# A two-layer attention and expert kernel: the expert table's bounds are read between pieces of expert 0, and the output table is cleared in two parts

## The chip, the core and the metric

One core of a Trainium2 chip runs the whole program in one launch. The metric is the device time of an execution in microseconds. Engines: PE is TensorE, DVE is VectorE, ACT is ScalarE, POOL is GpSimd, SP is SyncE, which only issues DMAs. A "q" behind an engine's name (ACTq, SPq, PEldq) stands for its sequencer, the part that takes instructions in order, does register work and passes the others on.

## The reference, cut to what matters

```
x = x + tanh(g_xattn[0]) * L0_xattn(layernorm(x), ctx)     # attention, 16 heads, 77 keys
x = x + tanh(g_ffn[0])   * L0_ffn(layernorm(x))            # 8 experts, each token goes to 2
x = x + tanh(g_xattn[1]) * L1_xattn(layernorm(x), ctx)
x = x + tanh(g_ffn[1])   * L1_ffn(layernorm(x))            # a Fourier-domain linear map

L0_ffn: probs = softmax(x @ gate_w.T); topw, sel = top_k(probs, 2); topw /= sum(topw)
        hact = up * gelu(gate)        # gate, up = x @ gate_up_w[e].T, 2 x 1024 columns
        out  = sum over the token's experts of topw * (hact @ down_w[e].T)
```

x is 16 batches of 256 rows of 256 numbers, so 4096 tokens; which expert gets how many is known only at run time.

## The kernel before, in words

**Layer 0.** Each engine runs a software pipeline over the 16 batches (`steps`). While a batch's attention runs, the one before gets its expert choice, and GpSimd scatters its rows (`scatter`, line 657) into the DRAM table `expert_in` (`xs_d`), where each expert has an area of its own. The DRAM table `expert_out` (`ys_d`, 14336 rows of 1 KB) takes the experts' results. It has to hold finite numbers everywhere, so SyncE clears it in layer 0: each of the 16 steps issues one DMA of 896 rows (`clear`, line 531) from the zeroed tile `zeros`. In SyncE's queue it stands behind `spread` and in front of `keep` (x1 to DRAM, line 554), `base` and `load`.

**The border.** VectorE counts the rows of each expert and writes `tbl`, one row of integers: the first tile of each expert (`bound`), where its whole tiles end and its half tiles begin (`end`), the row of its padding, and its first row in `expert_out` (`offset`); then it signals `tiles_counted` (line 1330). A whole tile is 256 rows, a half tile 128. Loops over tiles have bounds that must be in registers: `value_load` reads one number of `tbl` from SBUF into a register of one engine. In the kernel before, TensorE (lines 1791, 1793), ScalarE (965 to 970) and VectorE (1406 to 1409) each read all that they need for all 8 experts here, 16, 25 and 17 numbers, before their first tile. SyncE reads one padding row and issues `pad_first` (256 zero rows behind expert 0's rows, line 444), waits for all scatters and for `first_padded`, reads expert 0's three bounds (`tile_rows`, 570 to 572) and fetches the first tile (line 576).

**Experts.** A tile: TensorE turns it (`t_x`, line 1758, the transposes of line 1456), ScalarE writes its high half to 16-bit numbers (`x_hi`, line 926), VectorE the rest (`x_low`, line 1360). Then 8 pieces `fc`: `up` (line 1773, 12 matmuls), gelu on ScalarE (947), product and the split in two 16-bit parts on VectorE (1382, 1386, 1388), and two pieces later `down` (1786, 6 matmuls). The next tile is turned within this one, after piece 2's `up`. Within an expert's first two tiles ScalarE and VectorE also convert the next expert's weights, in parts (`next_high`, 938, behind the gelu of pieces 0 to 5 of the first tile; `next_low`, 1371, one for each of pieces 1 to 6 of both), and GpSimd fetches the weights of the one after that as stages come free. The first two tiles of an expert are written out one by one, the rest are loops over a register. The result rows go to `expert_out` from ScalarE's DMA queue (960, 963).

GpSimd, between layer 0 and its weight loop: after the first tile landed it fetches expert 1's down weights (line 737), after the second it runs `pad(pool, 1, E)`, seven DMAs of 256 zero rows. SyncE waits for these before expert 1's first tile.

After expert 7 layer 1 gathers rows from `expert_out` and goes on batch by batch; TensorE is its busiest engine too.

Of the kernel before, what the change touches and what calls it, by code (L numbers as in the profile page):

```python
# [26 lines left out]
P = 128  # L27
NB, S, D = 16, 256, 256
# [3 lines left out]
QT = S // P  # L32
HC = H // KC
E, F = 8, 1024
FC = F // P
TILES = 2 * NB + 4 * E
SHORT = 7
OUT_ROWS = (2 * NB + 3 * E) * S
CAP = NB * S + S
SCALE = 64.0  # L40
INV = 1.0 / SCALE
# [98 lines left out]
def build(nc, a, out):  # L140
# [27 lines left out]
    with ExitStack() as ctx:  # L168
# [3 lines left out]
        def sem(name):  # L172
            return ctx.enter_context(nc.semaphore(name))
# [178 lines left out]
        s.normed_after_turned = sem("normed_after_turned")  # L352
        s.normed_after_high = sem("normed_after_high")
        s.table_zeroed = sem("table_zeroed")
        s.logits = sem("logits")
        s.picked = sem("picked")
        s.prefix = sem("prefix")
# [120 lines left out]
        def _(sp):  # L478
# [51 lines left out]

            def clear(b):

                n = OUT_ROWS // NB
                dst = ys_d[bass.ds(b.i * n, n), :].rearrange("(p t) d -> p t d", p=P)
                sp.dma_start(dst, zeros[:, 0:1].to_broadcast([P, n // P, D])).then_inc(s.table_zeroed, 16)

            def step0(b, front, tail, pre, ld):
                if isinstance(b.i, int) and b.i == 1:
# [27 lines left out]
            keep(at(0, 15))  # L566


            def tile_rows(e):
                t0 = sp.value_load(tbl[0:1, bass.ds(e, 1)], min_val=0, max_val=TILES)  # L570
                t1 = sp.value_load(tbl[0:1, bass.ds(e + 1, 1)], min_val=1, max_val=TILES)
                tw = sp.value_load(tbl[0:1, bass.ds(e + (2 * E + 1), 1)], min_val=1, max_val=TILES)
                with sp.Fori(t0, tw) as g:
                    sp.wait_ge(s.tile_turned, g + 1)
                    row = tile_row(e, g, t0)
                    sp.dma_start(xs, rows(xs_d, row)).then_inc(s.tile_in, 16)
                with sp.Fori(tw, t1) as g:
                    sp.wait_ge(s.tile_turned, g + 1)
                    row = half_row(e, g, t0, tw)
                    sp.dma_start(xs[:, 0], xs_d[bass.ds(row, P), :]).then_inc(s.tile_in, 16)  # L580

            sp.wait_ge(s.tiles_counted, 1)
            pad_first(sp)
            for k in range(2):
                sp.wait_ge(s_scat[k], 64 * (NB // 2))
# [45 lines left out]
        def _(pool):  # L631
# [127 lines left out]
        def _(act):  # L759
# [182 lines left out]
            def expert_tile(e, g, par, part, first, t0, tw, n=QT):  # L942

                for fc in range(FC):
                    act.wait_ge(s.gate_up, g * FC + (fc + 1))
                    act.wait_ge(s.product, g * FC + (fc + 7))
                    act.activation(ge[:, fc % 2, 0:n * P], bank[1 + fc % 3][:, 0:n * P], ACT.Gelu,  # L947
                                   scale=INV).then_inc(s.gelu, 1)
                    if part == 0 and par is not None and fc < 6:
                        next_high(e, par, fc)  # L950
                x_hi(g + 1)
                act.wait_ge(s.down, g * FC + 2 * FC)
                act.wait_ge(s.expert_rows_stored, g * 16 + 16)
                for t in range(n):
                    act.activation(ysb[:, t], bank[4 + t][:, 0:D], ACT.Copy,
                                   scale=INV).then_inc(s.expert_rows, QT // n)
                act.wait_ge(s.expert_rows, g * 2 + 4)
                if n == QT:
                    row = out_row(first + (g * S - t0 * S), S)
                    act.dma_start(rows(ys_d, row), ysb).then_inc(s.expert_rows_stored, 16)  # L960
                else:
                    row = out_row(first + (g * P + tw * P - t0 * S), P)
                    act.dma_start(ys_d[bass.ds(row, P), :], ysb[:, 0]).then_inc(s.expert_rows_stored, 16)

            bound = [act.value_load(tbl[0:1, e:e + 1], min_val=4 if e else 0, max_val=TILES)
                     for e in range(E + 1)]
            end = [act.value_load(tbl[0:1, 2 * E + 1 + e:2 * E + 2 + e], min_val=3, max_val=TILES - 1)
                   for e in range(E)]
            offset = [act.value_load(tbl[0:1, 3 * E + 1 + e:3 * E + 2 + e], min_val=0,
                                     max_val=OUT_ROWS - SHORT * P) for e in range(E)]  # L970

            def expert(e, par):
                t0, t1, tw, first = bound[e], bound[e + 1], end[e], offset[e]
                expert_tile(e, t0, par, 0, first, t0, tw)
                expert_tile(e, t0 + 1, par, 1, first, t0, tw)
                with act.Fori(t0 + 2, tw) as g:
                    expert_tile(e, g, par, 2, first, t0, tw)
                with act.Fori(tw, t1) as g:
                    expert_tile(e, g, par, 2, first, t0, tw, 1)
# [34 lines left out]
        def _(dve):  # L1014
# [361 lines left out]
            def expert_tile(e, g, par, part, n=QT):  # L1376

                q = n * P
                done = part * (12 - sum(LOW_PIECES[1]))
                for fc in range(FC):  # L1380
                    dve.wait_ge(s.gelu, g * FC + (fc + 1))
                    dve.scalar_tensor_tensor(a32[:, fc % 2, 0:q], bank[1 + fc % 3][:, S:S + q], INV,  # L1382
                                             ge[:, fc % 2, 0:q], ALU.mult, ALU.mult).then_inc(s.product, 1)
                    dve.wait_ge(s.product, g * FC + (fc + 9))
                    dve.wait_ge(s.down, g * FC + (fc + 5))
                    dve.tensor_copy(act16[:, fc % 4, 0, 0:q], a32[:, fc % 2, 0:q]).then_inc(s.activation, 1)  # L1386
                    dve.wait_ge(s.activation, g * (2 * FC) + (2 * fc + 1))
                    dve.tensor_tensor(act16[:, fc % 4, 1, 0:q], a32[:, fc % 2, 0:q],  # L1388
                                      act16[:, fc % 4, 0, 0:q], ALU.subtract).then_inc(s.activation, 1)
                    if part < 2 and par is not None:  # L1390
                        for k in range(done, done + LOW_PIECES[part][fc]):
                            next_low(e, par, k)
                        done += LOW_PIECES[part][fc]
                x_low(g + 1)

            def expert(e, par):
                t0, t1, tw = bound[e], bound[e + 1], end[e]
                expert_tile(e, t0, par, 0)
                expert_tile(e, t0 + 1, par, 1)
                with dve.Fori(t0 + 2, tw) as g:  # L1400
                    expert_tile(e, g, par, 2)
                with dve.Fori(tw, t1) as g:
                    expert_tile(e, g, par, 2, 1)

            dve.wait_ge(s.tiles_counted, 1)
            bound = [dve.value_load(tbl[0:1, e:e + 1], min_val=4 if e else 0, max_val=TILES)
                     for e in range(E + 1)]
            end = [dve.value_load(tbl[0:1, 2 * E + 1 + e:2 * E + 2 + e], min_val=3, max_val=TILES - 1)
                   for e in range(E)]
            x_low(0)  # L1410
            for e in range(E - 1):
                expert(e, (e + 1) % 2)
# [38 lines left out]
        def _(pe):  # L1451
# [326 lines left out]
            def down(par, g, fc, w=QT):  # L1778
                if fc == 0:
                    pe.wait_ge(s.expert_rows, g * 2 + 2)  # L1780
                for n, (i, j) in enumerate(PASSES):
# [3 lines left out]
                    for t in range(w):  # L1785
# [5 lines left out]
            bound = [0] + [pe.value_load(tbl[0:1, e:e + 1], min_val=1, max_val=TILES)  # L1791
                           for e in range(1, E + 1)]
            end = [pe.value_load(tbl[0:1, 2 * E + 1 + e:2 * E + 2 + e], min_val=1, max_val=TILES)
                   for e in range(E)]
# [116 lines left out]
```

## Time and profile before

| | |
|---|---|
| median of 3 runs | 1301.15 us (1299.22 to 1301.48) |
| the profiled execution | 1300.25 us, its span 1298.7 us |
| TensorE's matmuls | 1189.8 us busy, 92% |
| VectorE / ScalarE / GpSimd | 69% / 44% / 20% |
| DMA over the span | 119.58 MB, 92 GB/s |
| layer 0 / experts / layer 1 | to about 380 / 380 to about 974 / to the end |

The profile is of one execution. Matmul ends are modelled, so a busy TensorE isn't TensorE at its peak. In a row such as `415.88 3.93 PE bank L1773 x36` the first number is the start in us from the span's start, the second the duration; `L1773` is the line of the kernel. `[0.31 <-DVE tiles L1386]` is idle time before an instruction and what ended it; "issue" is a wait for nothing that the profile shows. A row of a stretch, such as `410.00:415.00 5.00, 5.00 (x46) ...`, gives its length, the busy us of PE, PEld (weight loads), DVE, ACT and POOL with their instructions, TensorE's granted clock (1.00 is 2.4 GHz, 0.50 is 1.2 GHz), the DMA engines' busy share and GB/s.

### The profile page before, as it was taken

How to read it: one execution, taken by the hardware profiler on the slowest of the kernel's cores; microseconds unless marked ns; L12 is line 12 of the kernel's file. 1: busy time of each engine (PE TensorE's matmuls, PEld its weight loads, DVE VectorE, ACT ScalarE, POOL GpSimd, SP SyncE). 2: the span in 40 equal slices, each digit the busy share in tenths (PEclk: the TensorE clock that was granted, in tenths of full speed). 3: DMA queues.
4: the chain of work that ended last, by engine and by line, in shares of the span. 5: the costliest groups of instructions: out<-in, count | busy, mean ns of one | idle time of the engine just before them, and what ended most of it. 6: DMA issues, size and time to landing. Idle time of an engine off the chain costs nothing.

```text
span 1298.7 us, 34926 instructions
## 1 busy us (share of the span) xinstructions
PE 1189.8 (92%) x11816; PEld 992.6 (76%) x11816; DVE 892.5 (69%) x2696; ACT 569.6 (44%) x1184; POOL 263.2 (20%) x394
## 2 busy tenths in 40 slices
PE   4898989898867999999999999999997999999996
PEld 3677777776646888888888888888885777777774
DVE  4687677777645667675766767686565787787872
ACT  4565555555513242242424233242223665666652
POOL 5023242333331000000000000000004344444310
PEclk9899788888878999999999999999999999999998
DMA  9443333333433213021121313101012232222210
GB/s 293 183 162 107 117 116 124 128 101 110 150 133 138 91 37 127 33 95 61 71 94 38 122 34 126 34 25 46 26 47 81 66 93 87 81 82 85 82 34 21
DMA packets 82745, 119.58 MB, mean 92 GB/s; under 512 B 27326, under 2 KB 52558, under 8 KB 80589
## 3 DMA queue, kind: packets, MB, share of 16 engines
q1 hardware_dynamic: 64172, 60.32, 14.8%
q0 software_dynamic: 12848, 49.05, 11.3%
q10 hardware_dynamic: 5616, 8.78, 1.8%
q8 instruction: 66, 1.08, 0.3%
q14 instruction: 43, 0.34, 0.1%
HBM read 63.81 MB, written 47.58 MB: 86 GB/s over the span
## 4 chain that ended last, share of the span: by engine, by line
PE 80%; DVE 7%; issue 6%; SPq 2%; ACT 2%; DMA 1%; another core or an unknown queue 0%; POOL 0%; DVEq 0%; POOLq 0%; ACTq 0%
PE bank L1773 28%; PE bank L1786 14%; PE bank L1600 7%; PE bank L1534 6%; PE bank L1456 5%; PE bank L1587 3%; PE bank L1517 3%; PE bank L1519 3%; PE bank L1476 3%; PE bank L1540 2%; PE bank L1611 1%; DVE bm L1094 1%; PE bank L1598 1%; PE bank L1560 1%; PE bank L1502 1%
## 5 line engine op out<-in xcount | busy, mean ns | idle before, releaser
L1773 PE MATMUL bank<-tiles,we 128*128 128x256 f16 (+1 forms) x3744 | 392.6, 258 | 11.1 <-issue 10.2
L1773 PEld LDWEIGHTS bank<-tiles,we 128*128 128x128 f16 x3744 | 324.7, 98 | 51.1 <-issue 18.6
L947 ACT ACTIVATE tiles<-bank 128x256 f32<-128x256 f32 (+1 forms) x312 | 109.3, 353 | 330.9 <-PE bank L1773 312.2
L1786 PE MATMUL bank<-we,tiles 128*128 128x256 f16 x1608 | 223.5, 273 | 5.5 <-DVE tiles L1386 4.4
L1382 DVE SCALAR_TENSOR_TENSOR tiles<-bank,tiles 128x256 f32<-128x256 f32 (+1 forms) x312 | 120.2, 385 | 143.6 <-ACT tiles L947 138.6
L1786 PEld LDWEIGHTS bank<-we,tiles 128*128 128x128 f16 x1608 | 148.7, 98 | 40.8 <-DVE tiles L1386 17.0
L1534 PE MATMUL bank<-qT,kbd 128*128 128x256 f16 x960 | 161.6, 288 | 1.9 <-issue 1.2
L1094 DVE TENSOR_REDUCE bm<-bank 128x4 bf16<-128x308 f32 x256 | 118.2, 475 | 62.9 <-PE bank L1519 48.8
L471 DVE TENSOR_TENSOR pr<-pr 128x512 f16<-128x512 f32 x160 | 108.4, 682 | 30.9 <-ACT pr L809 25.0
L1388 DVE TENSOR_TENSOR tiles<-tiles 128x256 f16<-128x256 f32 (+1 forms) x312 | 121.1, 388 | 11.2 <-DVE tiles L1386 0.7
L1534 PEld LDWEIGHTS bank<-qT,kbd 128*128 128x128 f16 x960 | 97.4, 104 | 21.5 <-issue 1.8
L808 ACT ACTIVATE pr<-bank 128x512 f32<-128x512 f32 x160 | 95.9, 599 | 18.2 <-PE bank L1540 12.3
L1386 DVE CAST tiles<-tiles 128x256 f16<-128x256 f32 (+1 forms) x312 | 85.8, 275 | 24.6 <-DVE tiles L1382 0.2
L417 POOL TENSOR_TENSOR cell<-cell 1x1 f32<-1x1 f32 x81 | 24.4, 306 | 368.7 <-DMA expert_out<-tiles 167.8
L1517 PE MATMUL bank<-kbd,qT 128*128 128x308 f16 x256 | 79.2, 313 | 21.1 <-issue 9.4
L809 ACT ACTIVATE pr<-bank 128x512 f16<-128x512 f32 x160 | 96.8, 605 | 0.0
L1540 PE MATMUL bank<-mrhs,mhead 112*128 112x256 bf16 x320 | 92.1, 288 | 1.7
L1587 PEld LDWEIGHTS bank<-vbd,pr 128*128 128x128 f16 x1920 | 73.8, 99 | 16.5 <-issue 7.6
L1587 PE MATMUL bank<-vbd,pr 128*128 128x34 f16 (+1 forms) x1920 | 79.2, 185 | 7.5 <-issue 7.4
L1519 PE MATMUL bank<-bm,identb 128*128 128x308 bf16 x256 | 79.9, 316 | 0.9 <-issue 0.9
L668 POOL DMA_INDIRECT yg<-expert_out,slot x64 | 63.0, 985 | 35.8 <-issue 16.6
L657 POOL DMA_INDIRECT expert_in<-h,slot x64 | 64.5, 1008 | 20.9 <-issue 16.8
(196 smaller groups left out, 1678.2 us busy)
## 6 DMA issues: line engine op xcount, KB each, us to landing
expert_out<-zeros SPq DMA_DIRECT2D x16, 896.0 KB
wes<-in_guT POOLq DMA_DIRECT2D x9, 1024.0 KB, 5.1
tiles<-expert_in SPq DMA_DIRECT2D x29, 256.0 KB, 2.6
pr<-in_guT POOLq DMA_DIRECT2D x7, 1024.0 KB
yg<-in_dnT POOLq DMA_DIRECT2D x7, 1024.0 KB
expert_out<-tiles ACTq DMA_DIRECT2D x28, 256.0 KB, 2.3
expert_in<-zeros POOLq DMA_DIRECT2D x8, 640.0 KB, 13.0
xin<-in_x SPq DMA_DIRECT2D x16, 256.0 KB
```

The lines of the kernel that those rows point to most:

```text
L471: eng.tensor_tensor(pr[:, g, 1], pr32[:, (b.par + g) % 2], pr[:, g, 0], ALU.subtract).then_inc(low_done(b, g)[0], 1)
L947: act.activation(ge[:, fc % 2, 0:n * P], bank[1 + fc % 3][:, 0:n * P], ACT.Gelu, scale=INV).then_inc(s.gelu, 1)
L1094: dve.tensor_reduce(bm[:, t, MROW + 4 * q:MROW + 4 * q + 4], a_place(g).rearrange("p (h k) -> p h k", h=4), AX, ALU.max).then_inc(s.maxima, 1)
L1382: dve.scalar_tensor_tensor(a32[:, fc % 2, 0:q], bank[1 + fc % 3][:, S:S + q], INV, ge[:, fc % 2, 0:q], ALU.mult, ALU.mult).then_inc(s.prod ...
L1388: dve.tensor_tensor(act16[:, fc % 4, 1, 0:q], a32[:, fc % 2, 0:q], act16[:, fc % 4, 0, 0:q], ALU.subtract).then_inc(s.activation, 1)
L1517: pe.matmul(dst, qT[:, b.par, 0, q // 2, t * P:(t + 1) * P], kbd[:, b.par, 0, q // 2, 4 * (q % 2):4 * (q % 2) + 4], start=True, stop=False)
L1519: pe.matmul(dst, identb[:], bm[:, t, 0:S2].unsqueeze(1).to_broadcast([P, 4, S2]), start=False, stop=True).then_inc(s.top_scores, 1)
L1534: pe.matmul(b_s[(b.par + g) % 2][:, j * S:(j + 1) * S], kbd[:, b.par, ki, c].rearrange("p h k -> p (h k)")[:, start:start + P], qT[:, b.pa ...
L1540: return pe.matmul(b_s[(b.par + g) % 2][:, j * S:(j + 1) * S], mhead[:].rearrange("p h k -> p (h k)")[:, c * ROWS + start:c * ROWS + start ...
L1587: last = pe.matmul(dst, pr[:, g, pi, j * S + t * P:j * S + (t + 1) * P], vbd[:, b.par, c, vi, n0:n1].rearrange("p n d -> p (n d)"), start= ...
L1773: last = pe.matmul(bank[1 + fc % 3][:, half * S:half * S + w * P], gate_up[:, par, c, i, col:col + P], xT[:, j, c, 0:w * P], start=n == 0, ...
L1786: last = pe.matmul(bank[4 + t][:, 0:D], act16[:, fc % 4, i, t * P:(t + 1) * P], we[:, par, 2, j, fc * D:(fc + 1) * D], start=fc == 0 and n ...
```

## The change

It does three things. (1) `bound[0]` is the constant 0, and TensorE, VectorE and ScalarE read the other numbers one at a time by `next_bound()`, called between the pieces of expert 0's first two tiles. (2) SyncE reads expert 0's three bounds before `pad_first` instead of after the waits. (3) Layer 0 clears only the rows that expert 0 can write (17 x 256 = 4352), in 16 clears of 256 rows and one more after the steps; GpSimd issues the other 9984 rows as three DMAs of 3328 rows, after the second tile has landed and before its pads. ScalarE waits for these before expert 1.

```diff
+FIRST_ROWS = NB * S + S
+LATE_CLEARS = 3
 # SyncE
             def clear(b):
-                n = OUT_ROWS // NB
-                dst = ys_d[bass.ds(b.i * n, n), :].rearrange("(p t) d -> p t d", p=P)
-                sp.dma_start(dst, zeros[:, 0:1].to_broadcast([P, n // P, D])).then_inc(s.table_zeroed, 16)
+                sp.dma_start(rows(ys_d, b.i * S), zeros[:]).then_inc(s.table_zeroed, 16)
...
+            sp.dma_start(rows(ys_d, NB * S), zeros[:]).then_inc(s.table_zeroed, 16)
             sp.wait_ge(s.tiles_counted, 1)
+            first = tile_bounds(0)          # the three value_loads that stood in tile_rows
             pad_first(sp)
             for k in range(2):
                 sp.wait_ge(s_scat[k], 64 * (NB // 2))
             sp.wait_ge(s.first_padded, 16)
-            tile_rows(0)
+            tile_rows(0, first)
             sp.wait_ge(s.padding_zeroed, 16 * (E - 1))
             with sp.Fori(1, E) as e:
-                tile_rows(e)
+                tile_rows(e, tile_bounds(e))
 # GpSimd
             pool.wait_ge(s.tile_in, 32)
+            n = (OUT_ROWS - FIRST_ROWS) // LATE_CLEARS
+            for k in range(LATE_CLEARS):
+                dst = ys_d[FIRST_ROWS + k * n:FIRST_ROWS + (k + 1) * n, :].rearrange("(p t) d -> p t d", p=P)
+                pool.dma_start(dst, zeros[:, 0:1].to_broadcast([P, n // P, D])).then_inc(s.later_table_zeroed, 16)
             pad(pool, 1, E)
 # ScalarE
-            act.wait_ge(s.table_zeroed, 16 * NB)
+            act.wait_ge(s.table_zeroed, 16 * (NB + 1))
...
                     if part == 0 and par is not None and fc < 6:
                         next_high(e, par, fc)
+                    if e == 0 and part < 2:
+                        for _ in range(part + 1):
+                            next_bound()
...
-            bound = [act.value_load(tbl[0:1, e:e + 1], ...) for e in range(E + 1)]
-            end = [act.value_load(...) for e in range(E)]
-            offset = [act.value_load(...) for e in range(E)]
+            bound, end, offset = [0], [], []
+            def next_bound():               # offset[0..7], then bound[1..8], then end[0..7]
+                if len(offset) < E: ... offset.append(act.value_load(...))
...
             for e in range(E - 1):
+                if e == 1:
+                    act.wait_ge(s.later_table_zeroed, 16 * LATE_CLEARS)
                 expert(e, (e + 1) % 2)
 # VectorE, behind next_low of each piece; bound[1..8], then end[0..7]
+                    if e == 0 and part < 2:
+                        next_bound()
 # TensorE; bound[1..8], then end[0..7]
                 for fc in range(2, FC):
                     up(par, g, fc, w)
                     if fc == 2:
                         t_x(g + 1)
+                    next_bound()
                     down(par, g, fc - 2, w)
+                    next_bound()
                 down(par, g, FC - 2, w)
+                next_bound()
                 down(par, g, FC - 1, w)
+                next_bound()
```

## Rows read from the trace of the kernel before

**Rows 1.** The page's chain that ended last, shares of the span by engine.

```profile
PE 80%; DVE 7%; issue 6%; SPq 2%; ACT 2%; DMA 1%; another core or an unknown queue 0%; POOL 0%; DVEq 0%; POOLq 0%; ACTq 0%
```

**Rows 2.** The chain of waits at the border: start, duration (us), what.

```profile
380.69 0.29 SPq L570
...
382.40 0.04 SPq L573
...
382.83 2.56 DMA tiles<-expert_in
385.39 4.89 issue
390.28 1.11 PE bank L1456 x4
...
397.63 5.79 PE bank L1773 x36
```

**Rows 3.** By line, value_loads: count, ns min/median/max, first and last start (us).

```profile
L1791 PEldq TENSOR_LOAD <-tbl x8: 301/303/639, 379.4 to 384.4; - x8
L1793 PEldq TENSOR_LOAD <-tbl x8: 295/301/307, 385.0 to 389.6; - x8
L965 ACTq TENSOR_LOAD <-tbl x9: 274/281/482, 383.1 to 387.9; - x9
L1406 DVEq TENSOR_LOAD <-tbl x9: 297/304/547, 384.6 to 389.9; - x9
```

**Rows 4.** Timeline at the border: start, duration, engine, line, operation, out<-in, count.

```profile
378.30 0.20 SPq L445 DMA_DIRECT2D expert_in<-zeros  x1
...
379.24 3.72 PE L1750 MATMUL bank<-yg,pr 128*128 128x256 f32 x16 [0.69 <-ACT pr L917]
...
396.93 0.60 ACT L928 ACTIVATE tiles<-bank 128x512 f16<-128x512 f32 x1 [13.22 <-issue]
```

**Rows 5.** Expert 0's first tile: timeline, then busy time by engine in a stretch.

```profile
413.39 0.68 DVE L1371 SCALAR_TENSOR_TENSOR we<-pr,we 128x512 f16<-128x512 f32 x1
...
415.02 0.57 PEld L1786 LDWEIGHTS bank<-we,tiles 128*128 128x128 f16 x6 [0.31 <-DVE tiles L1386]
...
410.00:415.00 5.00, 5.00 (x46) 4.23 (x44) 4.66 (x12) 2.45 (x5) 0.54 (x1) 1.00 0.48 147
```

**Rows 6.** Third tile: down()'s first register work on the sequencer, its first matmuls.

```profile
L1784 PEldq FUSED_REGOPS  x1: 37/37/37, 434.8 to 434.8; - x1
...
436.63 0.82 PE L1786 MATMUL bank<-we,tiles 128*128 128x256 f16 x6
```

**Rows 7.** DMA issues: size, us to landing; and a stretch with the DMA engines full.

```profile
expert_in<-zeros SPq DMA_DIRECT2D x1, 256.0 KB, 1.8
wes<-in_guT POOLq DMA_DIRECT2D x9, 1024.0 KB, 5.1
we<-in_w SPq DMA_DIRECT2D x8, 256.0 KB, 8.8
...
31.00:43.00 12.00, 8.96 (x56) 6.97 (x57) 4.71 (x11) 2.56 (x5) 0.00 (x0) 0.72 1.04 397
```

**Rows 8.** TensorE's waits from 60 to 365 us, its only one for a DMA.

```profile
PE bank L1598 <- DMA brows<-we: 2.1, 1, 2.1
```

**Rows 9.** Chain of waits over experts 0 and 1, a fetch, and two stretches' granted clock.

```profile
415.88 3.93 PE bank L1773 x36
...
432.26 4.09 PE bank L1773 x36
...
468.80 11.86 SPq L576 DMA_DIRECT2D tiles<-expert_in  x2
...
475.48 4.10 PE bank L1773 x36
...
367.10:370.50 3.40, 1.96 (x14) 1.39 (x12) 0.00 (x0) 1.97 (x4) 2.79 (x3) 0.99 0.86 334
...
387.50:401.10 13.60, 4.58 (x21) 3.11 (x22) 0.69 (x1) 1.25 (x2) 2.21 (x4) 0.50 0.46 155
```

More of the change, by code:

```diff
@@ L354, in build @@
         s.table_zeroed = sem("table_zeroed")
+        s.later_table_zeroed = sem("later_table_zeroed")
         s.logits = sem("logits")
@@ L566, in _, with tile_bounds @@
             keep(at(0, 15))
-            def tile_rows(e):
+            def tile_bounds(e):
                 t0 = sp.value_load(tbl[0:1, bass.ds(e, 1)], min_val=0, max_val=TILES)
@@ L572, in tile_rows @@
                 tw = sp.value_load(tbl[0:1, bass.ds(e + (2 * E + 1), 1)], min_val=1, max_val=TILES)
+                return t0, t1, tw
+            def tile_rows(e, bounds):
+                t0, t1, tw = bounds
                 with sp.Fori(t0, tw) as g:
@@ L940, in next_high, with expert_tile @@
                                scale=SCALE).then_inc(s.next_high, 1)
-            def expert_tile(e, g, par, part, first, t0, tw, n=QT):
+            def expert_tile(e, g, par, part, t0, n=QT):
                 for fc in range(FC):
@@ L958, in expert_tile @@
                 if n == QT:
-                    row = out_row(first + (g * S - t0 * S), S)
+                    row = out_row(offset[e] + (g * S - t0 * S), S)
                     act.dma_start(rows(ys_d, row), ysb).then_inc(s.expert_rows_stored, 16)
                 else:
-                    row = out_row(first + (g * P + tw * P - t0 * S), P)
+                    row = out_row(offset[e] + (g * P + end[e] * P - t0 * S), P)
                     act.dma_start(ys_d[bass.ds(row, P), :], ysb[:, 0]).then_inc(s.expert_rows_stored, 16)
-            bound = [act.value_load(tbl[0:1, e:e + 1], min_val=4 if e else 0, max_val=TILES)
-                     for e in range(E + 1)]
@@ L967, in _ @@
[L967 to L970, printed above, removed]
-            def expert(e, par):
[L973 to L979, printed above, removed]
+            bound, end, offset = [0], [], []
@@ new lines, in next_bound @@
+            def next_bound():
+                if len(offset) < E:
+                    e = 3 * E + 1 + len(offset)
+                    offset.append(act.value_load(tbl[0:1, e:e + 1], min_val=0, max_val=OUT_ROWS - SHORT * P))
+                elif len(bound) <= E:
+                    e = len(bound)
+                    bound.append(act.value_load(tbl[0:1, e:e + 1], min_val=4, max_val=TILES))
+                elif len(end) < E:
+                    e = 2 * E + 1 + len(end)
+                    end.append(act.value_load(tbl[0:1, e:e + 1], min_val=3, max_val=TILES - 1))
@@ L981, in _ @@
+            def expert(e, par):
+                t0 = bound[e]
+                expert_tile(e, t0, par, 0, t0)
+                expert_tile(e, t0 + 1, par, 1, t0)
+                with act.Fori(t0 + 2, end[e]) as g:
+                    expert_tile(e, g, par, 2, t0)
+                with act.Fori(end[e], bound[e + 1]) as g:
+                    expert_tile(e, g, par, 2, t0, 1)
             x_hi(0)
             for e in range(E - 1):
+                if e == 1:
+                    act.wait_ge(s.later_table_zeroed, 16 * LATE_CLEARS)
@@ L1393, in expert_tile, with next_bound @@
                         done += LOW_PIECES[part][fc]
+                    if e == 0 and part < 2:
+                        next_bound()
                 x_low(g + 1)
             def expert(e, par):
-                t0, t1, tw = bound[e], bound[e + 1], end[e]
+                t0 = bound[e]
                 expert_tile(e, t0, par, 0)
                 expert_tile(e, t0 + 1, par, 1)
-                with dve.Fori(t0 + 2, tw) as g:
+                with dve.Fori(t0 + 2, end[e]) as g:
                     expert_tile(e, g, par, 2)
-                with dve.Fori(tw, t1) as g:
+                with dve.Fori(end[e], bound[e + 1]) as g:
                     expert_tile(e, g, par, 2, 1)
             dve.wait_ge(s.tiles_counted, 1)
[L1406 to L1409, printed above, removed]
+            bound, end = [0], []
+            def next_bound():
+                if len(bound) <= E:
+                    e = len(bound)
+                    bound.append(dve.value_load(tbl[0:1, e:e + 1], min_val=4, max_val=TILES))
+                elif len(end) < E:
+                    e = 2 * E + 1 + len(end)
+                    end.append(dve.value_load(tbl[0:1, e:e + 1], min_val=3, max_val=TILES - 1))
             x_low(0)
@@ L1789, in down, with next_bound @@
                 last.then_inc(s.down, 1)
[L1791 to L1794, printed above, removed]
+            bound, end = [0], []
+            def next_bound():
+                if len(bound) <= E:
+                    e = len(bound)
+                    bound.append(pe.value_load(tbl[0:1, e:e + 1], min_val=1, max_val=TILES))
+                elif len(end) < E:
+                    e = 2 * E + 1 + len(end)
+                    end.append(pe.value_load(tbl[0:1, e:e + 1], min_val=1, max_val=TILES))
             def tile(e, g, w):
```

## The prediction

> **What bounds the kernel now.** The page comes first. TensorE is on the last-ending chain for 80% of the span; "issue", time that nothing in the profile explains, is 6% [rows 1]. So the question is whether the change touches TensorE's own stretches or one of those holes. The chain of waits in order of time shows the largest hole, between layer 0 and expert 0 [rows 2]: the wait for the scatters is over when SyncE begins its reads at 380.69, the first tile is fetched (2.56 us from 382.83) and lands at 385.39, and then TensorE, with its data there, stands 4.89 us before the transposes at 390.28 (1.11 us) and 6.24 us more, 391.39 to 397.63, before the first expert matmul.
>
> The rows by line [rows 3] say what fills the hole: value_load. Each one is a TENSOR_LOAD of about 0.3 us with register work behind it. On TensorE 16 run from 379.4; the last starts at 389.6, and the transposes follow at 390.28: 0.66 us from one to the next (385.0 to 389.6, 7 steps). ScalarE reads 25 from 383.1 on and its x_hi starts at 396.93 [rows 4], 13.8/25 = 0.55 each. VectorE reads 17 from 384.6 on, 5.3/8 = 0.66 each, so until about 395.8. So the hole is one wait after another: TensorE's own reads to 390.3, then ScalarE's to 396.9.
>
> **The change, part by part.**
>
> *Reads leave the gap.* TensorE, ScalarE and VectorE read nothing before the first tile. What is late next? TensorE's product L1750 ends at 382.96 [rows 4]; ScalarE and VectorE are free for other things when their reads begin, 383.1 and 384.6 [rows 3]. All that is before the tile's data, so the tile decides, and SyncE's order is changed too. SyncE now reads expert 0's three bounds ahead of pad_first. These took from 380.69 to 382.40 (1.71 us) behind the scatter wait [rows 2]; they now stand in front of the pad's DMA, so that one goes from 378.30 [rows 4] to 380.01. It took 1.8 us to land [rows 7]: 381.8, later than the scatters (before 380.69), so first_padded becomes the wait that ends last. From the end of the reads to the issue it took 382.83 - 382.40 = 0.43; I take 0.5: tile DMA at 382.3, landed (2.56) at 384.9. SyncE's part is worth 0.5 us, not 1.7. Bounds: 0 to 1.7.
>
> Then transposes at 384.95 for 0.6 (they took 1.11 at 1.2 GHz in [rows 2]; TensorE has rested only 2 us here, so I halve that) to 385.6; x_hi at once; from x_hi's start to the first expert matmul it took 397.63 - 396.93 = 0.70. First matmul at 386.3. **Gain: 397.63 - 386.3 = 11.3 us.** VectorE's x_low follows x_hi as before.
>
> *Where the reads go.* TensorE gets 14 in expert 0's first tile, 2 in its second, between groups of 12 and 6 matmuls; VectorE 8 and 8; ScalarE 8 and 16 (24 in all, as bound[0] is now the constant 0).
>
> TensorE: L1791's first load starts at 379.4 while L1750's 16 matmuls run from 379.24 to 382.96 [rows 3, 4], so a read runs beside queued matmuls. How much is queued: the register operation for down()'s first wait of the tile that begins at 432.26 ran at 434.8, its first matmul at 436.63 [rows 6]: 1.8 us of lead, some 17 matmuls. Per piece of 18 matmuls (1.31 + 0.66 = 1.97 us [rows 9]) the two reads need 1.3 us of the sequencer. The rest, 0.7 us, must suffice to issue 18 matmuls and their weight loads; it does if the lead builds as fast as it must have between 432.26 and 434.8 (36 matmuls issued in 2.5 us while also stopped by a full queue). I take 0. Bounds: 0 (a read adds work and takes none away), and all 16 x 0.66 = 10.6 us exposed. The Trainium skill, TensorE: Matmul & The Clock Gate, section on the array's architectural detail, gives TensorE's queue a depth of 64; as 32 matmuls with their weight loads that would be nearly twice the lead of [rows 6], and it would make the cover safer; the trace bears out the smaller one.
>
> ScalarE: it is busy 2.45 of 5.00 us from 410 to 415 [rows 5], and a piece of 1.97 us leaves room for one read (0.55) in the first tile; in the second, without next_high, for two. At each tile's end the reads precede x_hi, which may move by up to 0.55 and 1.1 us. VectorE is the tight one: in the first tile it hardly idles, and down(7) already waits 0.31 for its cast [rows 5]. Behind next_low (0.68 [rows 5]) a read of 0.66 is hidden if VectorE's sequencer runs ahead as TensorE's does; in pieces 0 and 7 there is no next_low and it sticks out, I guess by half. I take 0.5 us for all this over both tiles. Bounds: 0, and 16 x 0.66 = 10.6.
>
> *Clears.* In layer 0 each of 16 clears shrinks from 896 KB to 256 KB, and a 17th comes after the last keep(), where SyncE has nothing to do before the counts are there (378.30 less the one read's time [rows 4]). From 60 to 365 us the only DMA that a compute engine waited for is the bias rows, 2.1 us once [rows 8]; nothing waits for clears. Worth 0, bounds 0 to 2.1. GpSimd now issues three clears of 3328 rows (9984 KB = 10.2 MB) after the second tile has landed (about 389), ahead of its seven pads and of expert 2's weights. With the DMA engines full they moved 397 GB/s [rows 7]: 26 us, so done about 416; at the pace of one 1 MB fetch by itself on that queue, 5.1 us [rows 7], it is 50 us, done about 439. The pads (1.8 MB, 5 to 8 us) follow. Their deadlines: SyncE needs the pads for expert 1's first tile, fetched at 468.80 [rows 9], now about 458; ScalarE's new wait, with all gelus of expert 1 and so TensorE behind it, stands at 475.48 - 11 = 464.5 [rows 9], where expert 2's weights are wanted too. Cost 0, cover 11 to 34 us. Tile transfers slow down beside it: 256 KB on SyncE's queue took 8.8 us when the DMA engines were full against 2.56 [rows 7, 2], and a tile has 16.4 us (415.88 to 432.26 [rows 9]). Cost 0.
>
> *Clock.* TensorE's clock fell to 1.2 GHz at 387.5 after its 382.96 to 387.5 rest and came back at 401.1, so 397.63 to 401.1 ran at half speed, 1.7 us lost [rows 9]. In the new order TensorE rests 2 us, transposes, rests 0.7 us. From 367.1 to 370.5 it was busy 1.96 of 3.40 us and 1.2 GHz followed [rows 9], so I expect about the same loss again: term 0. Bounds: -1.7 (it stays at 2.4 GHz) and +1.7 (twice as long).
>
> **Sum.** Profiled execution: span 1298.7, own time 1300.25. 1300.25 - 11.3 + 0.5 = 1289.4. The median of the three runs is 0.9 above that execution, so 1290.3 on its scale; I state 1290.0. Expert 0 to 7 and layer 1 follow in one chain on TensorE, so a shift at 397 arrives whole.
>
> **Rivals.**
> A. *Reads aren't hidden.* They push the pieces apart, on TensorE or on VectorE, which is nearly full in the first tile (4.66 of 5.00 us from 410 to 415 [rows 5]). On TensorE wholly: +10.6, 1300.0, within 0.2% of before. On VectorE wholly: 8 x 0.66 = 5.3 in a tile, less the 0.34 in 5 us that it idles and some slack behind the two pieces by which down() lags, I guess 1.5, twice, about +7: 1297. Half hidden: 1294. For: 14 of 16 sit in one tile. Against: the first read at 379.4 [rows 3], in the middle of L1750's matmuls. Chance 0.15.
> B. *The gap closes only in part*, as another late party keeps 3 us of it (pad_first slower beside the scatters, or expert 1's 1 MB of down weights, issued when the first tile has landed, delaying the second tile that t_x(1) wants at 390.3). Second tile: issued 385.7, 2.6 alone 388.3, 5.1 as a 1 MB transfer 390.8: +0.5; at 8.8, 394.5: +4. Time 1290.5 to 1294. Chance 0.09.
> C. *Slower.* Place: GpSimd's queue. 12 MB (clears and pads) stand ahead of expert 1's first tile. Needed by 458 from 389, so 174 GB/s; below it TensorE stands at the end of expert 0, and from 12 MB / (458 + 11 - 389 = 80 us) = 150 GB/s down the whole is slower than before. At 100 GB/s: 120 us, ends 509, stall 51, time 1341. For: clears and pads are issued to one queue. The Trainium skill, DMA: Bandwidth & Descriptors, section on queues, rings and completion order, says that a ring is consumed in order, so the pads could not overtake; no row here shows such a case. Against: the same kind of zero copy on the same queue ran when 397 GB/s were moved [rows 7]. Chance 0.04.
> D. *No effect*: the tile waits elsewhere and all is as before, 1301. Nothing in the rows speaks for it. Chance 0.02.
>
> **Numbers.** Forecast case 0.70, A 0.15, B 0.09, C 0.04, D 0.02. A change under 0.2% (2.6 us) can't be told from none. Forecast case and B are faster, A in a bit over half of its cases: 0.87; same: 0.08; slower: 0.05. Range: the forecast's own is 1287.5 to 1292; stretched over B and half of A to 1297, down to 1287 for a clock that stays up and reads that cost nothing.
>
> **What would show it.** First expert matmul near 386 instead of 397.6, the pad's DMA near 380.0, TENSOR_LOADs in the first tile with TensorE's groups of 12 matmuls still 1.31 us long, both tiles still 16.4 us long (the first less any clock loss), clears done before 435, expert 1 starting near 464.7. Wrong if the first tile is over 1.5 us longer beyond its clock loss, if the start is later than 388, or if TensorE waits at the border to expert 1.

## The result and the profile after

| | before | after |
|---|---|---|
| median | 1301.15 us (13 runs in all: 1296.03 to 1304.1) | 1297.03 us (13 runs: 1293.42 to 1298.85) |
| ratio | | 0.9968, 95% interval 0.9955 to 0.998 |
| the profiled execution, its span | 1300.25, 1298.7 us | 1295.19, 1293.6 us |

The change makes the kernel 0.3% faster: about 4 us, where I had forecast 11. The median is 0.03 us outside my range (1287 to 1297), but the gain is little more than a third of the one forecast. Below, a clear is one of the DMAs that zero rows of `expert_out`, and the late clears are the three that GpSimd issues.

The chain of waits at the border (start, duration, what) is the first thing to look at; it answers to [rows 2]:

```profile
377.84 1.99 DMA expert_in<-zeros
380.36 2.52 DMA tiles<-expert_in
384.46 0.70 DVE tiles L1384
385.21 4.04 PE bank L1803 x20
```

and TensorE's timeline for expert 0's first tile and the start and end of its second (`L1803` is `up`, L1773 before; `L1816` is `down`):

```profile
377.29 3.72 PE L1780 MATMUL bank<-yg,pr 128*128 128x256 f32 x16 [0.69 <-issue]
383.01 0.63 PE L1486 MATMUL bank<-cst,tiles 128*128 128x128 f32 x4 [2.00 <-DMA tiles<-expert_in]
384.45 0.60 PE L1803 MATMUL bank<-tiles,we 128*128 128x256 f16 x4 [0.81 <-issue]
...
394.30 1.48 PE L1803 MATMUL bank<-tiles,we 128*128 128x256 f16 x12 [0.50 <-DVE tiles L1404]
397.26 1.48 PE L1803 MATMUL bank<-tiles,we 128*128 128x256 f16 x12 [0.76 <-DVE tiles L1404]
...
408.24 4.09 PE L1803 MATMUL bank<-tiles,we 128*128 128x256 f16 x36 [0.77 <-issue]
...
425.29 0.85 PE L1816 MATMUL bank<-we,tiles 128*128 128x256 f16 x6 [0.87 <-DVE tiles L1408]
427.01 0.85 PE L1816 MATMUL bank<-we,tiles 128*128 128x256 f16 x6 [0.87 <-DVE tiles L1408]
427.86 0.39 PE L1803 MATMUL bank<-tiles,we 128*128 128x256 f16 x2
```

The border is as forecast. From the start of layer 0's last product to the first expert matmul it took 379.24 to 397.63, 18.39 us [rows 2, 4]; now 377.29 to 384.45, 7.16 us: 11.2 us gained. But the first tile lasts 408.24 - 384.45 = 23.8 us instead of 18.25, and the second, to 427.87, 19.6 instead of 16.38 [rows 9]. That gives back 5.5 + 3.3 = 8.8 us. The two together leave 2.4 us. The span is 5.1 us shorter, as layer 0 also ended 1.95 us earlier in this execution and 0.7 us lies behind the second tile. In the first tile a piece that had come every 1.97 us [rows 9] comes after 2.96 us (394.30 to 397.26), with TensorE idle in front of each. In the second the pieces keep their pace until the end, where each `down` waits for VectorE's cast.

The rows by line say why (count, ns min/median/max, first and last start in us); they answer to [rows 3]. TensorE and VectorE, then ScalarE in the first tile, in the second tile, and at its end:

```profile
L1826 PEldq TENSOR_LOAD <-tbl x8: 899/966/1227, 388.7 to 398.6; - x8
L1829 PEldq TENSOR_LOAD <-tbl x8: 940/961/990, 400.0 to 412.1; - x8
L1435 DVEq TENSOR_LOAD <-tbl x8: 792/960/1066, 388.5 to 405.4; - x8
L984 ACTq TENSOR_LOAD <-tbl x8: 477/941/1229, 386.8 to 404.2; - x8
L987 ACTq TENSOR_LOAD <-tbl x8: 892/918/1299, 409.8 to 418.8; - x8
L990 ACTq TENSOR_LOAD <-tbl x8: 274/282/857, 420.1 to 425.6; - x8
```

The same instruction took a median of 0.28 to 0.30 us in the kernel before. It takes 0.92 to 0.97 us from 388 us on and is back at 0.28 within L990's eight. In the trace the late clears have landed by 400.2, 408.9 and 419.3, and the seven pads, behind them on the same queue, by 424.7. The last slow loads start at 421.16 (857 ns), 421.26 (880) and 422.36 (661), when only pads are left of these DMAs; from 423.27 on they take 0.27 to 0.31 us. First the issues of the late clears (number, KB each, us to landing), then stretches (us, busy time of PE, PEld, DVE, ACT, POOL, TensorE's granted clock, DMA share, GB/s):

```profile
expert_out<-zeros POOLq DMA_DIRECT2D x3, 3328.0 KB, 20.1
```

```profile
388.00:396.00 8.00, 7.47 (x62) 5.87 (x61) 6.12 (x14) 4.32 (x8) 4.45 (x6) 0.94 1.01 369
...
404.00:412.00 8.00, 6.23 (x55) 4.90 (x54) 2.99 (x7) 2.02 (x5) 1.08 (x2) 1.00 1.02 385
...
423.00:427.00 4.00, 2.13 (x16) 0.98 (x14) 3.80 (x11) 1.36 (x3) 0.04 (x1) 1.00 0.92 386
```

In the last stretch the same queue of GpSimd brings expert 2's weights from DRAM to SBUF, as many bytes per second as the clears move, and the loads are fast.

With 0.96 us for the load and the same register work behind it, a read costs TensorE's sequencer some 1.35 us (its loads start 1.31 us apart and more), two make 2.7, and a piece is 1.97 us of matmuls. The cover is too short by 0.7 us a piece, and the pieces come every 2.65 to 2.96 us.

### The profile page after: what moved, and what is told of

Same layout as the page of the kernel before. It is cut to its first block, busy times and chain, and to the rows that moved or that the text cites. A ratio compares the mean times of both kernels' runs of the same rounds, so it can differ in the third digit from the quotient of the medians.

```text
span 1293.6 us, 34855 instructions
## 1 busy us (share of the span) xinstructions
PE 1188.4 (92%) x11816; PEld 989.0 (76%) x11816; DVE 892.7 (69%) x2696; ACT 570.4 (44%) x1184; POOL 267.1 (21%) x397
## 4 chain that ended last, share of the span: by engine, by line
PE 79%; DVE 9%; issue 6%; ACT 2%; DMA 2%; ACTq 1%; SPq 1%; DVEq 0%; another core or an unknown queue 0%; POOL 0%; POOLq 0%
PE bank L1803 27%; PE bank L1816 13%; PE bank L1630 7%; PE bank L1564 6%; PE bank L1486 5%; PE bank L1617 3%; PE bank L1547 3%; PE bank L1506 3%; PE bank L1549 3%; PE bank L1570 2%; PE bank L1641 1%; PE bank L1524 1%; DVE bm L1116 1%; PE bank L1628 1%; PE bank L1590 1%
## 5 line engine op out<-in xcount | busy, mean ns | idle before, releaser
L1803 PE MATMUL bank<-tiles,we 128*128 128x256 f16 (+1 forms) x3744 | 392.9, 258 | 8.9 <-issue 5.5
L1803 PEld LDWEIGHTS bank<-tiles,we 128*128 128x128 f16 x3744 | 324.1, 98 | 50.6 <-issue 14.3
L1816 PE MATMUL bank<-we,tiles 128*128 128x256 f16 x1608 | 223.9, 273 | 8.7 <-DVE tiles L1408 7.1
L1816 PEld LDWEIGHTS bank<-we,tiles 128*128 128x128 f16 x1608 | 147.9, 98 | 45.8 <-DVE tiles L1408 19.7
## 6 DMA issues: line engine op xcount, KB each, us to landing
expert_out<-zeros POOLq DMA_DIRECT2D x3, 3328.0 KB, 20.1
```

The costliest lines, as they stand in the source:

```text
L1803: last = pe.matmul(bank[1 + fc % 3][:, half * S:half * S + w * P], gate_up[:, par, c, i, col:col + P], xT[:, j, c, 0:w * P], start=n == 0, ...
L1816: last = pe.matmul(bank[4 + t][:, 0:D], act16[:, fc % 4, i, t * P:(t + 1) * P], we[:, par, 2, j, fc * D:(fc + 1) * D], start=fc == 0 and n ...
```

## The experiments

Several chips took part. In the runs of the result, and beside e9 to e11, the kernel before took about 1300 us; beside e1 to e8 it took 1240.8, with TensorE's granted clock 0.98 on average against 0.95. These last are two sets, e1 to e4 on one chip and e5 to e8 on another. So only runs beside each other are compared, and tiles by their lengths. Tile 1 and 2 are expert 0's first two, from `up`'s first matmul to that of the next tile.

| kernel | median, runs | against before, 95% | tile 1 + tile 2 |
|---|---|---|---|
| before (the result's runs) | 1301.15 | | 18.25 + 16.38 |
| changed (the result's runs) | 1297.03, 13 | 0.9955 to 0.998 | 23.8 + 19.6 |
| before, beside e1 to e4 and beside e5 to e8 | 1240.75, 17 and 1240.80, 17 | | |
| e1 reads only | 1226.34, 6 | 0.9858 to 0.991 | 18.8 + 16.5 |
| e2 clears only | 1240.38, 12 | 0.9983 to 1.0017 | 17.9 + 16.5 |
| e3 clears after the reads | 1228.74, 6 | 0.9882 to 0.9934 | 18.8 + 16.9 |
| e5 changed again | 1237.25, 12 | 0.9959 to 0.9989 | 23.1 + 20.4 |
| e7 reads only again | 1228.49, 6 | 0.9876 to 0.9917 | 18.8 + 16.5 |
| e8 pad before the reads | 1225.84, 6 | 0.9866 to 0.991 | 17.1 + 16.5 |

e4, e6 (1237.64 us) and e9 to e11 ran once each, so their times settle nothing and only their profiles are used.

My theory after the result: the late clears slow every read of a bound while they run, and so uncover reads that would be hidden (theory 1). The rival: reads placed between pieces are slow by themselves, the engines being busy, whatever GpSimd issues (theory 2).

**e1, the reads moved, all clears in layer 0 as before.** The 17th clear, GpSimd's three and ScalarE's wait for them are gone too.

```diff
-                sp.dma_start(rows(ys_d, b.i * S), zeros[:]).then_inc(s.table_zeroed, 16)
+                n = OUT_ROWS // NB
+                dst = ys_d[bass.ds(b.i * n, n), :].rearrange("(p t) d -> p t d", p=P)
+                sp.dma_start(dst, zeros[:, 0:1].to_broadcast([P, n // P, D])).then_inc(s.table_zeroed, 16)
```

> The reads and SyncE's order as in the changed kernel, the clears all in layer 0 as before. In the changed kernel a TENSOR_LOAD between pieces takes 0.95 us, not 0.30, and expert 0's first two tiles take 23.8 and 19.6 us. Theory 1: the three late clears slow the loads. Then loads take 0.3 here, the tiles 16.4 to 18.3 us, and the time is 11 us below before, about 1290. Theory 2: a load is slow because TensorE, ScalarE and VectorE are all busy. Then loads take 0.95 here too and the time is that of the changed kernel, 1297, or a little above.

Measured: 14.4 us faster than before (ratio 0.9884), where 11 were expected. The two tiles took 35.2 us, 0.8 us more than in e2, which reads before them on the same chip. TensorE's first eight loads had a median of 0.35 us, and no read was on the chain:

```profile
L1821 PEldq TENSOR_LOAD <-tbl x8: 296/348/699, 335.7 to 342.3; - x8
```

**e2, the clears moved, the reads where they were before** (the edit is against the changed kernel). SyncE reads in `tile_rows` again; TensorE, VectorE and ScalarE read all their numbers before their first tile.

```diff
-            first = tile_bounds(0)
             pad_first(sp)
...
-            tile_rows(0, first)
+            tile_rows(0)
```

> The clears as in the changed kernel (17 small ones in layer 0, three from GpSimd in expert 0), the reads and SyncE's order as before. Both theories: the reads are over before the clears start, loads of 0.3, so within 0.5 us of before. If the smaller clears make layer 0 shorter (the changed kernel's last product of layer 0 started 1.95 us earlier), about 1299.

Measured: no difference (0.9983 to 1.0017). The engines had read at 0.30 us before the clears began; GpSimd, which reads its pads' rows beside the clears, had 0.95 us, where in the kernel before the same seven reads took 0.30. The rows of before, then those of e2:

```profile
L439 POOLq TENSOR_LOAD <-tbl x7: 287/297/507, 394.5 to 403.8; - x7
```

```profile
L1799 PEldq TENSOR_LOAD <-tbl x8: 297/306/594, 323.1 to 327.9; - x8
L442 POOLq TENSOR_LOAD <-tbl x7: 849/947/1264, 340.8 to 354.3; - x7
```

So moving the clears by itself is worth and costs nothing that these runs can tell (the interval is 2 us each way); the loss is in the two together.

**e3, the changed kernel, with GpSimd's late clears behind the pads and expert 2's weights**, when the reads are over.

```diff
+            pad(pool, 1, E)
+            for part in range(3):
+                pool.wait_ge(s.expert_weights, 2 * 3 - 3 + (part + 1))
+                fetch(2, part, part)
             n = (OUT_ROWS - FIRST_ROWS) // LATE_CLEARS
...
-            pad(pool, 1, E)
-            with pool.Fori(2, E) as e:
+            with pool.Fori(3, E) as e:
```

> The changed kernel, but GpSimd issues its three clears behind the pads and behind expert 2's weights, so when all reads are done. Theory 1: loads 0.3 us, tiles 16.4 to 18.3 us, clears done near 450, before expert 1 at 464; time 1288 to 1290. Theory 2: as the changed kernel, 1297.

Measured: 12.0 us faster than before (0.9908), the tiles short again. Same work, same queue, another time: the loss is gone. It isn't better than e1 either, so clearing late shows no gain of its own. The clears reach a fifth engine here: SyncE's three reads for expert 1 fall among them, and their loads, otherwise 0.27 us, took 0.91, 0.96 and 1.24 us (369.28 to 371.95).

**e4, e1 and three copies from DRAM to DRAM** of the clears' size, issued by GpSimd where the changed kernel issues its clears; ScalarE waits for them before expert 1, as it does there for the clears. This asks whether full DMA engines are enough.

```diff
+            n = (OUT_ROWS - FIRST_ROWS) // LATE_CLEARS
+            for k in range(LATE_CLEARS):
+                src = a["guT"].rearrange("r (u d) -> (r u) d", d=D)[k * n:(k + 1) * n, :].rearrange("(p t) d -> p t d", p=P)
+                dst = copy_d[k * n:(k + 1) * n, :].rearrange("(p t) d -> p t d", p=P)
+                pool.dma_start(dst, src).then_inc(s.later_table_zeroed, 16)
```

> As the kernel with the reads only, plus three DMAs of 3328 KB each from GpSimd at the place of the late clears, which copy weights from DRAM to a DRAM scratch table: as many bytes, but nothing read from SBUF. ScalarE waits for them before expert 1. If any full load of the DMA engines slows a value_load: loads near 0.95 us while they run. If only DMAs that read SBUF do: 0.3. Theory 2: 0.95 in either case, before and after the copies too.

Measured: one run, 1239.91 us. TensorE's loads stayed at 0.30 us though the DMA engines were full (a stretch's row as above):

```profile
L1832 PEldq TENSOR_LOAD <-tbl x8: 296/298/308, 343.4 to 363.5; - x8
```

```profile
338.00:362.00 24.00, 15.68 (x141) 13.26 (x138) 15.58 (x36) 7.70 (x15) 4.91 (x9) 0.92 1.00 334
```

So neither the DMA share nor writing to DRAM slows a load by itself. What made this kernel slow is another thing, on the chain of waits: a tile's fetch of 256 KB, usually 2.6 us, took 24.8, and TensorE stood for it.

```profile
337.87 24.77 DMA tiles<-expert_in
```

**e5, the changed kernel again**, beside e7, which is e1 again. No edit.

> The changed kernel unaltered, so that it and the same kernel with all clears in layer 0 are timed beside one another. Theory 1 (the late clears slow each read of a bound from 0.30 to 0.95 us while they run): the first two tiles of expert 0 are together 7 to 9 us longer than in the kernel with all clears in layer 0, the first matmul of expert 0 within 1 us of it, and the median is 7 to 9 us above it; TENSOR_LOADs of 0.9 us and more until the clears have landed. Theory 2 (reads between busy engines are slow by themselves): no difference over 2 us between the two.

> The changed kernel with all 16 clears of 896 rows in layer 0, as before the change, run beside the changed kernel itself. Theory 1: 7 to 9 us faster than the changed kernel and 12 to 15 us faster than the kernel before; TENSOR_LOADs 0.28 to 0.37 us in the first two tiles outside the pads. Theory 2: as the changed kernel.

Measured: 1237.25 and 1228.49 us. The late clears cost 8.8 us, as theory 1 had it (7 to 9). Tiles 1 and 2 are together 43.5 us in e5 (330.09 to 373.57) and 35.2 in e7 (333.05 to 368.28): 8.3 us, nearly all of it. The first expert matmul was to be within 1 us in both and wasn't: e5's is 3.0 us earlier, as its layer 0 ended 2.75 us earlier, and behind the second tile e5 took 2.3 us longer. Both differ by as much between other single executions here. e5's loads had medians of 0.92 to 0.98 us, but for ScalarE's last eight, in which they came back to 0.28; e7's:

```profile
L1824 PEldq TENSOR_LOAD <-tbl x8: 297/300/477, 345.3 to 355.0; - x8
L1433 DVEq TENSOR_LOAD <-tbl x8: 301/304/311, 354.5 to 367.4; - x8
```

**e6, the late clears read partitions 64 to 127 only**, `tbl` being in partition 0.

```diff
-                pool.dma_start(dst, zeros[:, 0:1].to_broadcast([P, n // P, D])).then_inc(s.later_table_zeroed, 16)
+                pool.dma_start(dst, zeros[P // 2:P, 0:1].to_broadcast([P // 2, n // (P // 2), D])).then_inc(s.later_table_zeroed, 16)
```

> The late clears take their zeros from partitions 64 to 127 alone; tbl lies in partition 0. If the loads are slow because the clears read the same part of SBUF as tbl, TENSOR_LOADs are back at 0.28 to 0.35 us while the clears run, and the first two tiles take about 18 and 16.5 us. If any DMA that reads SBUF slows them, wherever it reads, they stay at 0.9 us or more and the tiles at 23 and 19 us. I hold the second the likelier, 0.6 to 0.4.

Measured: the loads stay slow, at a DMA rate of 222 GB/s instead of 385. The clears now take 36 us to land instead of 20, and the second tile grew to 22.7 us (350.38 to 373.11).

```profile
L1826 PEldq TENSOR_LOAD <-tbl x8: 504/1019/1048, 330.9 to 340.4; - x8
L987 ACTq TENSOR_LOAD <-tbl x8: 909/986/1014, 351.9 to 360.8; - x8
```

```profile
340.00:356.00 16.00, 12.97 (x108) 9.65 (x106) 7.77 (x19) 4.12 (x9) 2.71 (x5) 1.00 0.99 222
```

So neither the bytes per second nor the reading of `tbl`'s own partition decide. What is common to the slow cases here is a DMA that reads SBUF. The fast ones were DRAM to DRAM (e4) and weights from DRAM to SBUF: at 386 GB/s in the changed kernel's stretch from 423 to 427 above, on GpSimd's queue like the clears.

**e9, e10, e11: whose slow reads?** In each the changed kernel does one engine's reads before its first tile, as before the change; the late clears stay. The kernel before took 1298.94 beside them. TensorE's edit (e9) is shown; ScalarE's (e10, `3 * E` reads) and VectorE's (e11) are alike, without the wait.

```diff
+            pe.wait_ge(s.tiles_counted, 1)
+            for _ in range(2 * E):
+                next_bound()
             t_x(0)
```

> The changed kernel, late clears and all, but TensorE does its 16 reads before it turns the first tile, as before the change; ScalarE and VectorE read between pieces. It tells whose slow reads lengthen the tiles. If TensorE's own carry the loss (2 reads of 1.13 us each and piece, 2.3 us, against 1.97 us of matmuls, in the first tile), the first tile is down by 3 to 4 us, to that of the kernel with all clears in layer 0, and the second stays up by 3, being ScalarE's. If VectorE's or ScalarE's carry it, the first stays over 2 us too long.

> The changed kernel with ScalarE's 24 reads before its first x_hi, as before the change; TensorE and VectorE read between pieces. If the second tile's loss is ScalarE's (two reads of 1.1 us behind every gelu; the chain of waits goes through them), the second tile is back at 16.4 to 17 us and the first stays at about 23. If VectorE's one read a piece carries it, the second tile stays over 18.5 us. The first matmul comes later by ScalarE's reads, as before.

> The changed kernel with VectorE's 16 reads before its first x_low; TensorE and ScalarE read between pieces. VectorE was 93% busy in the first tile, so by my rival A in the prediction its reads should be the costly ones: then both tiles come back by 2 us and more. If TensorE and ScalarE carry the loss, the tiles stay at about 23 and 19.5 us.

e9, 1299.48 us: the first tile's pieces follow at 1.97 us again, without an idle moment. Its end and the second tile don't. The timeline:

```profile
404.81 1.47 PE L1803 MATMUL bank<-tiles,we 128*128 128x256 f16 x12
406.12 0.82 PE L1816 MATMUL bank<-we,tiles 128*128 128x256 f16 x6
406.78 1.47 PE L1803 MATMUL bank<-tiles,we 128*128 128x256 f16 x12
...
409.50 0.85 PE L1816 MATMUL bank<-we,tiles 128*128 128x256 f16 x6 [0.59 <-DVE tiles L1408]
411.58 0.85 PE L1816 MATMUL bank<-we,tiles 128*128 128x256 f16 x6 [1.24 <-DVE tiles L1408]
412.27 0.60 PE L1803 MATMUL bank<-tiles,we 128*128 128x256 f16 x4
413.64 5.33 PE L1803 MATMUL bank<-tiles,we 128*128 128x256 f16 x32 [0.76 <-DVE tiles L1384]
```

The two tiles together (391.32 to 434.11) are 42.8 us, 20.95 and 21.8, against 43.4 in the changed kernel. But part of that is the clock. TensorE had rested 7.6 us for its reads before it turned the first tile, and 2.6 us in all, in three pauses, between 408.9 and 413.7; the granted clock was 0.50 both times:

```profile
386.40:396.60 10.20, 6.39 (x29) 4.29 (x30) 1.93 (x4) 3.21 (x4) 2.41 (x2) 0.50 0.48 156
...
413.70:417.10 3.40, 3.40 (x17) 2.35 (x18) 1.08 (x3) 0.38 (x1) 0.00 (x0) 0.50 1.01 382
```

So 5.3 us of e9's first tile (391.3 to 396.6) and 3.4 us of its second ran at half speed, which costs half of each, 2.7 and 1.7 us. In the changed kernel it was 3.4 us of the first tile, so 1.7, and none of the second. By this estimate e9's tiles would be 18.3 and 20.1 us at full speed, the changed kernel's 22.1 and 19.6. So in the first tile's pieces TensorE's reads are the bound, and without them 3.8 us come back there, as expected (3 to 4). The second tile gains nothing: there VectorE and ScalarE are late. Of the 8.8 us some 3.3 go with TensorE's reads, the rest stays with those of the other two engines.

e10, 1310.96 us: the gap opened, as ScalarE's 24 reads ran into the clears, the last nine at about 0.93 us; its first tile was 23.2 us, and its second 16.5. e11, 1301.96 us: VectorE's reads also ran into them and held the first tile; they are on the chain of waits up to 395.8:

```profile
390.80 0.93 DVEq L1438
392.04 0.99 DVEq L1438
```

The first tile, from its fifth matmul on, then took 23.4 us still (396.66 to 420.07), against 23.0 in the changed kernel (385.21 to 408.24), with only TensorE and ScalarE reading in it; the second took 16.5. In both the second tile proves less than I wanted: the first tile having begun later, clears and pads were over before it in e10 and by its fourth microsecond in e11, and all its loads in e10 and most in e11 took 0.27 to 0.31 us. What these two show is that TensorE's pieces in the first tile stay 2.6 to 3.3 us apart (once 2.2, at the start of e11's) with either VectorE's or ScalarE's reads gone. Their 23 us hold more half speed than the changed kernel's, until 409.3 and 402.3, so 2.4 and 2.8 us lost against 1.7: without it they are 1.3 and 0.7 us shorter than its first tile. No run isolates the second tile. In the changed kernel's the trace speaks for ScalarE: the chain goes through its reads, and VectorE stands in front of its product in every piece but the last two until ScalarE's gelu is there (the last two rows):

```profile
410.93 0.92 ACTq L987
413.35 0.92 ACTq L987
415.75 1.12 ACTq L987
```

```profile
415.01 0.42 DVE L1404 SCALAR_TENSOR_TENSOR tiles<-bank,tiles 128x256 f32<-128x256 f32 x1 [0.61 <-ACT tiles L958]
...
420.45 0.42 DVE L1404 SCALAR_TENSOR_TENSOR tiles<-bank,tiles 128x256 f32<-128x256 f32 x1 [1.03 <-ACT tiles L958]
```

**e8, all clears in layer 0 and the pad's DMA before SyncE's reads** (the edit is against e7).

```diff
             sp.wait_ge(s.tiles_counted, 1)
-            first = tile_bounds(0)
             pad_first(sp)
+            first = tile_bounds(0)
```

> All clears in layer 0 as in the kernel before it in this list, and SyncE issues pad_first first and reads expert 0's three bounds behind it, still ahead of the waits for the scatters. The pad's DMA starts at once instead of behind three reads and lands while they run. The reads took 1.7 us and the pad 2 us to land, so the tile's fetch should start about 1.3 us earlier, unless the scatters are the later wait; then 0 to 1. Expected 0.5 to 1.5 us faster than its neighbour, first expert matmul earlier by the same.

Measured: 1225.84 against e7's 1228.49, 2.6 us less, where 0.5 to 1.5 were expected, and the lowest median here; the intervals of their ratios overlap, so the medians don't settle it. The chain shows what the new order does: the scatter (DMA expert_in<-h,slot) is now the last to land, so more isn't to be had from the pad.

```profile
319.74 2.74 DMA expert_in<-h,slot
...
322.99 2.65 DMA tiles<-expert_in
...
327.97 3.67 PE bank L1798 x32
```

From the start of layer 0's last product to the tile's fetch it took 3.22 us in e7 (325.62 to 328.84) and 2.06 in e8 (320.93 to 322.99): 1.2 us. In this execution the clock gave more. TensorE stood 1.13 us instead of 2.27 before it turned the tile, and 32 of the matmuls behind it took 3.67 us instead of 5.29: it kept the full clock and saved another 1.6. That this follows from the shorter rest isn't shown: e4 kept the full clock behind a rest of 1.98 us (the same 32 matmuls took 3.67), and e6, behind 1.95, did not (5.33).

## Why the prediction was wrong, step by step

- **The gap: right.** 11.3 us forecast, 11.2 measured; pad's DMA 377.84 (380.0 forecast, with this run's layer 0 ending 1.95 us earlier), the pad last of the waits, as said. Whether that early end is an effect of the change is open: in e1 to e8 the last product began at 319.6 to 322.9 us in the four kernels with the small clears in layer 0 and at 320.9 to 325.6 in the four with the large ones, and e2's median is no lower for it. By the medians the gain is 4.1 us, 1.7 more than 11.2 less 8.8; their interval allows 2.6 to 5.9.
- **The reads in the tiles: this step failed.** I wrote that two reads "need 1.3 us of the sequencer" and took 0 for TensorE and 0.5 us for all. The cover was there, as e1 and e7 show, where the same reads cost little at 0.30 us each (the two tiles are 0.6 us longer than before, 0.8 longer than e2's). The price was not: it was read off in a stretch in which no late clear ran, and used in one in which three did. The load measured 0.96 us, the read 1.35, and the term 8.8 us instead of 0.5, inside the bound of 10.6 that I had kept.
- **The clears: right on their deadlines, wrong in kind.** They landed by 419.3 and the pads by 424.7, well before anything waited for them, and rival C's mechanism didn't appear; e2's difference is 0. ([rows 8] show TensorE's waits only; the trace shows no such wait of another compute engine in that time either.) But I priced them at 0 only by who waits for them, not by what runs beside them. The loss is an interaction of the two parts that I costed one by one: 0 for the clears alone (e2), 0.6 to 0.8 for the reads alone (e1's tiles), and 8.8 more for both together (e5 less e7).
- **Rival A** had the mechanism, with 0.15: TensorE's reads push the pieces apart; 1297 is between its 1294 and 1300. That the time falls there is in part luck, as 1.7 us of the gain came from neither the gap nor the tiles. Its reason, that the engines have no room, was not the cause: the room was there until the load tripled. I had also placed VectorE as the tight one; e9 and e11 say TensorE in the first tile's pieces.
- **The clock: right for the changed kernel** (3.4 us at half speed, until about 389, where it had been 3.5), but e4 and e8 show that the bound of -1.7 is real: there the clock stayed up behind rests of 2.0 and 1.1 us, though in e6 it fell behind one of 1.95.

## What to carry to other kernels

A duration read from a trace belongs to what ran beside it. When a change moves a small operation in time, or moves a large transfer beside it, look up what the operation costs next to such a transfer, and cost the parts of a change together as well as one by one. Put work with no deadline where nothing short and serial runs: here the clears belong in layer 0 or behind the reads.

## What the runs showed of the hardware

- A register load from SBUF (TENSOR_LOAD) took 0.28 to 0.30 us, and a median of 0.9 to 1.03 us on all of TensorE, VectorE, ScalarE and GpSimd (SyncE in e3: 0.91 to 1.24) while DMAs moved 10 MB from SBUF to DRAM, at 385 GB/s and at 222 GB/s alike, and whether these read partition 0 or not. Copies from DRAM to DRAM at 334 GB/s (e4) and weights from DRAM to SBUF at 386 GB/s (the changed kernel, 423 to 427) left it at about 0.30. Reading SBUF is the common feature of the slow cases; no run took the mechanism apart. The Trainium skill, Runtime: NRT & Kernel Launch, section on instruction fetch mechanics, describes a load of a register from HBM as a round trip over AXI of about 200 ns, and SBUF — State Buffer, section on SBUF's two sides, puts the DMAs' ports to SBUF on the same fabric. The 0.28 to 0.30 us here are for loads from SBUF. That these go over the same fabric and meet the DMAs there is a guess that would fit both; no run here shows where they meet, and DMAs that write SBUF didn't slow them. The same section says that DMAs and compute operations can't slow each other; for register loads beside DMAs that read SBUF the measurement here says otherwise.
- Seven pads of 256 KB, which read SBUF too, slow it less or for a shorter time: issued one by one they went with single loads of 0.5 to 0.7 us (e1, e7), which the first load of a series takes elsewhere too (639 ns in [rows 3]); landing back to back behind the clears (419.3 to 424.7 in the changed kernel) they gave 0.66 to 0.88 us.
- Beside DRAM to DRAM copies on GpSimd's queue a 256 KB fetch on SyncE's took 24.8 us; beside the clears from SBUF no fetch was on the chain.
